# Decoder kernel: routing and scattering three of four token chunks inside the attention stream, expert tiles in fixed places, late expert weights on another queue, banded layer-norm gain applied elsewhere

## The chip, the core and the metric

The kernel runs on one core of one Trainium2 chip. The metric is the device time of one execution in microseconds (us); three executions of the kernel before were timed. TensorE (PE) multiplies matrices from SBUF into PSUM, VectorE (DVE) and ScalarE (ACT) do elementwise work and reductions, GpSimd (POOL) does elementwise work and issues the indirect transfers, SyncE (SP) issues the other transfers. PEld is PE's weight load. Each engine runs its own list of instructions in order; engines wait for one another by semaphores.

## The reference

Two decoder layers over 2048 tokens of width 256, each with self-attention, cross-attention over a context of 1601 tokens, a feed-forward block, and a layer norm after each. What matters here is the end of the first block, and the mixture of experts that closes the second layer.

```python
# layer 0, banded attention: layer norm with gamma and beta, then a GELU block
x = _layernorm(x + attn, gamma, beta)          # (x - mu) * rsqrt(var + eps) * gamma + beta
x = x + (gelu(x @ W1 + b1) @ W2 + b2)
...
# layer 1: mixture of 8 experts, the best 2 for every token
scores = x_flat @ gate_w + gate_b
topk_vals, topk_idx = jax.lax.top_k(scores, 2)
topk_probs = jax.nn.softmax(topk_vals, axis=-1)
h = jax.nn.relu(einsum('td,edf->etf', x_flat, w1) + b1[:, None, :])
y = einsum('etf,efd->etd', h, w2) + b2[:, None, :]
out = einsum('te,etd->td', combine_w, y)       # combine_w holds topk_probs
x = _layernorm(x + out)
```

Counted from the reference's inputs, its router sends 122, 34, 1250, 277, 133, 461, 1088 and 731 tokens to experts 0 to 7: 1, 1, 10, 3, 2, 4, 9 and 6 tiles of 128 rows, 36 in all.

## The kernel before

**Tiling.** Tokens stand in 16 tiles of 128 (`NT`), four tiles to a chunk (`QT`, `NQ` = 4). `x_tok` holds them row by row, `x_fm` column by column (features on the partitions). Stages follow one another as blocks, with a barrier of all engines between two blocks.

**Banded attention (layer 0).** At its end SP runs `behind(sp)`, here `clear_slots` (L2602): one transfer writes zeros into `x_slots`, which has 39 tiles of 128 rows in device memory (`EXPERT_TILES`). The block `close_attention` (L1006 to L1100) follows: product with `Wo`, residual, and a `RowNorm` (L222 to L260). On DVE `scale` normalises a tile (L239) and multiplies by gamma and adds beta (L243, L245); PE turns it (L252), ACT copies it to `x_fm` (L258). POOL adds the bias beforehand (L1037). The next block, `gelu_ffn`, loads its weights on SP (L1841 to L1844).

**The stream (`decoder_attention`).** Both attentions of layer 1 run as one stream of (score tile, key tile) pairs. `Plan` writes out its order by hand: `places` spreads the searches for row maxima (PE L1294, DVE L1307), which run 5 pairs ahead, `tasks[p]` holds the small jobs done after pair p, and `close_chunks` sets a chunk's closing jobs some pairs behind its last step. Products for maxima and all small jobs share a ring of four PSUM banks (`set_ring`); a product waits (`bank_free`) until the user four places earlier has been read. Per pair PE makes four score products (L1483), ACT their exponentials (L1624), PE the product with the values (L1499). The last 13 pairs have no maxima beside them. At the stream's start DVE and ACT wait for five loads (`s_w`, 80); POOL waits for `s_wo` and then prepares 16 residual tiles (L1692, L1695) before it does unit 0's cast (L1711), for which DVE waits at L1779.

**Routing and placing.** After the stream `route` (L1932 ff.) computes logits for 16 tiles (PE L1970, DVE L2001 to L2006) and the gates; SP loads the biases and `EARLY_EXPERTS` = 3 experts of 2 MB each. Then `place_tokens` (L2202 ff.) counts by prefix sums over 32 columns which slot each token takes (DVE chain L2251 to L2293, each link waiting for the one before), and POOL issues 32 indirect scatters of one column each (L2308) into `x_slots`; SP loads experts 3 to 7 meanwhile.

**Experts (`expert_ffn`).** 39 tiles in a hardware loop. For tile i SP loads 128 rows from `x_slots` (L2385), PE turns them (`turn_x`, L2413), multiplies by the first weight (`up`, L2424), turns (L2435) and multiplies by the second (`down`, L2443); DVE adds the bias (L2528), SP stores to `y_slots` (L2389). In one round SP issues load(i + 2) once `turn_x(i + 1)` is done and then waits for the bias of tile i to store it, so load(i + 3) stands behind that store. PE, ACT and DVE read the tile's expert number from SBUF into a register (`expert_of`, L2380). `up` waits for `s_resident`, which POOL raises expert by expert as the weights land. At the end POOL gathers both outputs of each token (L2503) and DVE sums them.

## Time and profile before

| | us |
|---|---|
| median of 3 runs | 3147.39 (3145.82 to 3147.58) |
| profiled execution, device time | 3147.17 |
| its span in the profile | 3145.4 |
| stream, first exponential to last copy into `x_fm` | 1298.8 to 2688.3 |
| routing and placing, up to the first row load | 2688.3 to 2769.5 |
| expert tiles, first `up` to last `down` | 2772.9 to 3090.9 |
| gather, sum, norm, output | 3091.0 to 3145.4 |

The profiled execution took 0.2 us less than the median. Its span is 1.8 us shorter than its device time, which holds what lies around it. The page gives PE as busy for 88% of the span, DVE 65%, ACT 52%, POOL 9%; these are averages over stages with different limits.

### The profile page before, as it was taken

How to read it: one execution, taken by the hardware profiler on the slowest of the kernel's cores; microseconds unless marked ns; L12 is line 12 of the kernel's file. 1: busy time of each engine (PE TensorE's matmuls, PEld its weight loads, DVE VectorE, ACT ScalarE, POOL GpSimd, SP SyncE). 2: the span in 40 equal slices, each digit the busy share in tenths (PEclk: the TensorE clock that was granted, in tenths of full speed). 3: DMA queues.
4: the chain of work that ended last, by engine and by line, in shares of the span. 5: the costliest groups of instructions: out<-in, count | busy, mean ns of one | idle time of the engine just before them, and what ended most of it. 6: DMA issues, size and time to landing. Idle time of an engine off the chain costs nothing. (4 is left out here: it accounts for less than half of the span.)

```text
span 3145.4 us, 85995 instructions
## 1 busy us (share of the span) xinstructions
PE 2774.2 (88%) x35706; PEld 1386.0 (44%) x35707; DVE 2054.1 (65%) x4240; ACT 1625.6 (52%) x3050; POOL 267.5 (9%) x381
## 2 busy tenths in 40 slices
PE   6796978999996988799999999999999999379992
PEld 3574643444543553233333333333343433247662
DVE  4444138888844236688898998989998994412224
ACT  2232213666662222277777777877777778023331
POOL 2113011000110001300000000000000000210003
PEclk9897988999997998699999999999999999589996
DMA  5412033011001004221212211111111110711112
GB/s 157 122 44 94 0 106 80 18 24 39 3 2 37 1 11 133 74 59 48 56 38 48 62 50 39 45 45 55 45 45 45 45 45 2 261 43 32 33 33 89
DMA packets 114947, 173.62 MB, mean 55 GB/s; under 512 B 19946, under 2 KB 90491, under 8 KB 114211
## 3 DMA queue, kind: packets, MB, share of 16 engines
q1 hardware_dynamic: 108772, 160.02, 17.8%
q0 software_dynamic: 5824, 8.49, 0.9%
q8 instruction: 272, 4.46, 0.6%
q14 instruction: 79, 0.65, 0.1%
HBM read 127.63 MB, written 40.51 MB: 53 GB/s over the span
## 5 line engine op out<-in xcount | busy, mean ns | idle before, releaser
L1307 DVE TENSOR_REDUCE d_part_max<-d_ps_m 128x1 f32<-128x512 f32 (+1 forms) x1964 | 1124.8, 630 | 86.4 <-PE d_ps_m L1294 53.3
L1624 ACT ACTIVATE d_prob<-d_ps_s 128x512 f32<-128x512 f32 x1856 | 960.2, 603 | 253.9 <-PE d_ps_s L1483 244.1
L1483 PE MATMUL d_ps_s<-q_st,k_st 98*32 98x512 bf16 x5104 | 445.2, 385 | 30.7 <-ACT d_prob L1624 28.8
L1294 PE MATMUL d_ps_m<-k_st,q_st 97*32 97x512 bf16 (+1 forms) x5296 | 471.9, 362 | 0.0
L698 DVE TENSOR_REDUCE x_part_max<-x_att_ps_m 128x1 f32<-128x512 f32 (+2 forms) x578 | 307.8, 586 | 43.3 <-PE x_att_ps_m L683 17.2
L939 ACT ACTIVATE x_att_prob<-x_att_ps_s 128x1024 f32<-128x1024 f32 (+3 forms) x296 | 258.2, 921 | 131.2 <-PE x_att_ps_s L820 78.2
L1499 PE MATMUL d_ps_o<-d_prob,a_values 128*32 128x512 f32 x2048 | 266.1, 595 | 0.0
L1483 PEld LDWEIGHTS d_ps_s<-q_st,k_st 98*32 98x32 bf16 x5104 | 136.3, 96 | 286.8 <-ACT d_prob L1624 182.6
L1294 PE MATMUL d_ps_m<-q_st 97*32 97x512 bf16 (+1 forms) x2560 | 227.6, 361 | 0.0
L1294 PEld LDWEIGHTS d_ps_m<-k_st,q_st 97*32 97x32 bf16 x5296 | 140.9, 96 | 178.8 <-issue 71.3
L1499 PE MATMUL d_ps_o<-d_prob,x_values 128*32 128x512 f32 x1664 | 215.3, 593 | 0.2 <-ACT d_prob L1624 0.2
L1483 PE MATMUL d_ps_s<-q_st 98*32 98x512 bf16 x2320 | 201.9, 382 | 8.6 <-ACT d_prob L1624 8.4
L674 PE MATMUL x_att_ps_m<-k_st,q_st 97*32 97x512 bf16 (+3 forms) x2312 | 203.5, 343 | 3.9 <-DVE x_part_max L698 3.0
L820 PE MATMUL x_att_ps_s<-q_st,k_st 98*32 98x512 bf16 (+3 forms) x2368 | 193.7, 357 | 12.0 <-DMA q_st<-x_neg_row 6.3
L2477 ACT ACTIVATE l1f_h_cols<-l1f_ps_t,l_b 128x128 f32<-128x128 f32 x312 | 84.7, 382 | 136.3 <-PE l1f_ps_t L2435 136.3
L2424 PE MATMUL l1f_ps_h<-l_w,l1f_x_cols 128*128 x312 | 143.3, 603 | 1.4 <-issue 0.7
L2443 PE MATMUL l1f_ps_y<-l_w,l1f_h_cols 128*128 x624 | 141.3, 379 | 2.2 <-ACT l1f_h_cols L2477 2.2
L853 PE MATMUL x_att_ps_o<-x_att_prob,v_grp 128*32 128x512 f32 (+3 forms) x1184 | 140.1, 543 | 0.4 <-ACT x_att_prob L939 0.4
L2522 DVE COPY l1f_h_rows<-l1f_ps_h 128x512 f32<-128x512 f32 x78 | 54.0, 692 | 127.3 <-PE l1f_ps_h L2424 127.3
L2443 PEld LDWEIGHTS l1f_ps_y<-l_w,l1f_h_cols 128*128 128x128 f32 x624 | 115.6, 190 | 17.0 <-issue 2.9
L1483 PEld LDWEIGHTS d_ps_s<-q_st 98*32 98x32 bf16 x2320 | 61.6, 96 | 120.7 <-ACT d_prob L1624 72.2
L1294 PEld LDWEIGHTS d_ps_m<-q_st 97*32 97x32 bf16 x2560 | 67.9, 96 | 86.7 <-issue 32.9
(328 smaller groups left out, 3342.5 us busy)
## 6 DMA issues: line engine op xcount, KB each, us to landing
k_st<-parts_k SPq DMA_DIRECT2D x90, 256.0 KB, 5.2
k_st<-parts_k SPq DMA_DIRECT2D x90, 208.0 KB, 4.7
l_w<-in_l_w SPq DMA_DIRECT2D x16, 1024.0 KB, 13.3
q_st<-parts_q SPq DMA_DIRECT2D x48, 256.0 KB, 4.7
q_st<-parts_q SPq DMA_DIRECT2D x192, 64.0 KB
q_st<-parts_k SPq DMA_DIRECT2D x30, 256.0 KB
q_st<-parts_k SPq DMA_DIRECT2D x30, 208.0 KB
parts_q<-a_proj_parts SPq DMA_DIRECT2D x16, 384.0 KB, 2.5
```

The source lines that it names most:

```text
L674: mm = pe.matmul(out[q:q + COLUMNS, :], q_st[0:rows, slot, j, start:start + COLUMNS], k_st[0:rows, slot, j, k:k + w], start=(half == 0), s ...
L698: dve.tensor_reduce(self.part[:, h * QT + a, i:i + 1], bank[:, 0:w], AX.X, ALU.max).then_inc(s_read, 1)
L820: mm = pe.matmul(bank[q:q + COLUMNS, hh, q0:QC], k_st[0:ROW_MAX + 1, bass.ds(slot(g), 1), h, key:key + COLUMNS], q_st[0:ROW_MAX + 1, bass. ...
L853: mm = pe.matmul(ps_o[32 * j:32 * j + 32, q0:QC], v_grp[:, kt, j, :], prob[:, k % 2, j, q0:QC], start=(i == 0), stop=(i == n - 1), skip_gr ...
L939: act.activation(prob[:, k % 2, 2 * u:2 * u + 2, q0:QC], bank[:, :, q0:QC], ACT.Exp, scale=scale).then_inc(s_prob, 1)
L1294: mm = pe.matmul(bank[q:q + COLUMNS, 0:w], self.query(s, h, ROW_MASK + 1, a * P + q, COLUMNS), self.key(s, h, ROW_MASK + 1, k, w), start=T ...
L1307: dve.tensor_reduce(self.part[:, h * QT + a, i:i + 1], bank[:, 0:w], AX.X, ALU.max).then_inc(s_read, 1)
L1483: mm = pe.matmul(ps_s[n % len(ps_s)][k:k + COLUMNS, :], maxima.key(s, h, ROW_MAX + 1, kt * P + k, COLUMNS), maxima.query(s, h, ROW_MAX + 1 ...
L1499: mm = pe.matmul(ps_o[32 * j:32 * j + 32, :], value_block(segments[si].values, kt, g * GH + j), prob[:, p % 2, j, :], start=(i == 0), stop ...
L1624: act.activation(prob[:, p % 2, h, :], ps_s[n % len(ps_s)][:, :], ACT.Exp, scale=scale).then_inc(s_prob, 1)
L2424: mm = pe.matmul(ps_h[hh][:, :], x_cols[:, m, :], w1_sb[:, bass.ds(e, 1), m, hh * QC:(hh + 1) * QC], start=(m == 0), stop=(m == DT - 1))
L2443: mm = pe.matmul(ps_y[:, 0:D], h_cols[:, f, :], w2_sb[:, bass.ds(e, 1), f, :], start=(f == 0), stop=(f == FT - 1))
```

## The change

- **Routing in the stream.** A class `Router` holds the gate weights and the counters. For chunks 0 to 2 the plan adds a `gate` task (PE logits of four tiles, DVE choice of two experts), three pairs later a `count` task (two products on PE, a prefix sum of 8 columns on DVE), and 8 `scatter` tasks on POOL, one every three pairs. The last chunk is done in a new block `dispatch` after the stream, with its 8 scatters. `route` and `place_tokens` go for layer 1.
- **Fixed places.** Each expert has 16 tiles of its own in `x_slots` (136 tiles with 8 spare ones, `SLOT_TILES`), so slots need no total. The zeros are written over 136 tiles. `expert_ffn` reads for each tile a row number from `tile_row` in SBUF, on SP, before each load and each store. Outputs go back into `x_slots`.
- **Weights.** SP loads experts 0 and 1 in `dispatch`. Experts 2 to 7 (12 transfers of 1 MB) are issued by POOL in `expert_ffn`, after the second row load has landed and before POOL raises `s_resident` for the first time.
- **Gain.** In the banded block PE turns the tile before gamma and beta. ACT applies them in its copy (two instructions of 128 columns, scale and bias per partition). POOL applies them to the rows with two operations per tile, after the turn. SP's zeros stand in its queue ahead of `gelu_ffn`'s weights, as before.
- **Waits.** In the stream DVE and ACT wait for `s_w` only at unit 0.

On PE, in the stream of the second attention, at the last chunk closed inside it. `x_tok` is turned for `x_fm` one job earlier; `d_ps_m` are the four ring banks. Before:

```order
L1294 MATMUL d_ps_m<-k_st,q_st 32x512 x4
L1509 MATMUL d_ps_m<-ident,d_o_raw 128x128 x4
L1483 MATMUL d_ps_s<-q_st 32x512 x4
...
L1499 MATMUL d_ps_o<-d_prob,x_values 32x512 x4
L1294 MATMUL d_ps_m<-k_st,q_st 32x128 x4
L1294 MATMUL d_ps_m<-k_st,q_st 32x512 x4
L1483 MATMUL d_ps_s<-q_st 32x512 x4
```

The same place in the changed kernel:

```order
L1313 MATMUL d_ps_m<-k_st,q_st 32x512 x4
L1663 MATMUL d_ps_m<-ident,d_o_raw 128x128 x4
L1637 MATMUL d_ps_s<-q_st 32x512 x4
...
L1653 MATMUL d_ps_o<-d_prob,x_values 32x512 x4
L1313 MATMUL d_ps_m<-k_st,q_st 32x128 x4
L1313 MATMUL d_ps_m<-k_st,q_st 32x512 x4
L1409 MATMUL d_ps_m<-router_w,x_fm 128x8 x8
L1637 MATMUL d_ps_s<-q_st 32x512 x4
```

Eight products for logits stand before the next pair's scores; the two count products stand three pairs later.

On SP, in the loop over the expert tiles, from the loop's start to its store. ISA and REGISTER_ALU are register instructions. Before:

```order
L2395 ISA
L2385 ISA
L2385 DMA l1f_x_rows<-x_slots 128x256
L2388 REGISTER_ALU
L2389 ISA
L2389 DMA y_slots<-l1f_y_rows 128x256
L2395 REGISTER_ALU
L2395 COMPARE_AND_BRANCH
```

In the changed kernel:

```order
L2568 ISA
L2546 TENSOR_LOAD l_tile_row
L2546 ISA x2
L2557 REGISTER_ALU
L2558 ISA
L2558 DMA l1f_x_rows<-x_slots 128x256
...
L2563 DMA x_slots<-l1f_y_rows 128x256
L2568 REGISTER_ALU
L2568 COMPARE_AND_BRANCH
```

A load from SBUF into a register and its two followers stand between the loop's start and the row load.

On POOL, in the expert block, before the gathers. In the changed kernel:

```order
L2486 DMA l_w<-in_l_w 128x2x1024
L2487 DMA l_w<-in_l_w 128x8x256
...
L2678 DMA l1f_y_two<-x_slots,router_slots 128x256 x32
```

Six such pairs of weight transfers stand there; before, POOL's list had only the 32 gathers.

The diff, cut to its core:

```diff
+SLOT_TILES = E * NT + E
@@ RowNorm
-            if self.gain is not None:
-                dve.wait_ge(self.s_x, 3 * t + 1)
-                dve.tensor_tensor(x, x, self.gain[:, 0, :], ALU.mult).then_inc(self.s_x, 1)
-                dve.wait_ge(self.s_x, 3 * t + 2)
-                dve.tensor_tensor(x, x, self.gain[:, 1, :], ALU.add).then_inc(self.s_x, 1)
+    def apply_gain(self, pool, t):
+        x = self.x_tok[:, t, :]
+        pool.wait_ge(self.s_turn, t + 1)
+        pool.tensor_tensor(x, x, self.gain[0][:, 0, :], ALU.mult).then_inc(self.s_gain, 1)
+        pool.wait_ge(self.s_gain, 2 * t + 1)
+        pool.tensor_tensor(x, x, self.gain[0][:, 1, :], ALU.add).then_inc(self.s_gain, 1)
...
+            for m in range(DT):
+                done = act.activation(self.x_fm[:, m, t * P:(t + 1) * P], self.ps[t % 2][:, m * P:(m + 1) * P],
+                                      ACT.Identity, scale=self.gain[1][:, 0, m:m + 1], bias=self.gain[1][:, 1, m:m + 1])
@@ Plan.close_chunks
+            if si == 1 and c < NQ - 1:
+                self.tasks[start + 14].append(("gate", c))
+                self.tasks[start + 17].append(("count", c))
+                for i in range(2 * QT):
+                    self.tasks[start + 19 + 3 * i].append(("scatter", c, i))
@@ Router, on VectorE: choose after the logits, place after the counts
+        dve.tensor_tensor(self.logit[:, :, :], bank[:, 0:self.LOGITS].rearrange("p (a e) -> p a e", e=E), ...
+        link(*(dve.max(self.best[:, a, :], self.logit[:, a, :]) for a in range(QT)))
+        link(*(dve.max_index(self.index[:, a, :], self.best[:, a, :], self.logit[:, a, :]) for a in range(QT)))
...
+        while w < C:
+            dst = self.upto[:, side, :, :]
+            link(dve.tensor_copy(dst[:, 0:w, :], src[:, 0:w, :]),
+                  dve.tensor_tensor(dst[:, w:C, :], src[:, w:C, :], src[:, 0:C - w, :], ALU.add))
@@ dispatch, on GpSimd
             pool.wait_ge(s_slots, 1)
-            pool.wait_ge(s_zero, 16)
-            for c in range(C):
-                pool.indirect_dma_start(x_slots, bass.IndirectOffsetOnAxis(slots[:, c:c + 1], 0),
-                                        x_tok[:, c // 2, :], None).then_inc(s_scatter, 16)
+            for i in range(2 * QT):
+                router.scatter(pool, c, i)
-EARLY_EXPERTS = 3
+EARLY_EXPERTS = 2
@@ expert_ffn
+        def rows(queue, dram, i):
+            row = queue.value_load(tile_row[0:1, bass.ds(i, 1)], min_val=0, max_val=SLOT_TILES - 1)
+            return dram[bass.ds(row * P, P), :]
...
             with sp.Fori(0, N - 2) as i:
-                sp.wait_ge(s_xturn, i + 2)
-                load(i + 2)
+                load(i + 2, i + 2)
                 store(i)
...
             pool.sem_inc(s_y, 1)
             pool.sem_inc(s_stored, 16)
+            pool.wait_ge(s_row, 32)
+            load_late(pool)
             for e in range(E):
                 pool.wait_ge(s_expert[e], 32)
                 pool.sem_inc(s_resident, 1)
@@ clear_slots
-                         cst["zeros"][:, :].rearrange("p (o n) -> p o n", o=1).to_broadcast((P, EXPERT_TILES, D)))\
+                         cst["zeros"][:, :].rearrange("p (o n) -> p o n", o=1).to_broadcast((P, SLOT_TILES, D)))\
```

## Rows read from the trace of the kernel before

**Rows 1.** Timeline after the stream: start, us, engine, line, operation, names, count, idle before
```profile
2687.03 1.24 ACT L1647 ACTIVATE x_fm<-d_ps_m 128x256 f32<-128x256 f32 x3 [0.19 <-PE d_ps_m L1544]
...
2693.04 13.82 PE L1970 MATMUL l1r_ps<-l1r_w,x_fm 128*128 128x8 f32 x64 [5.19 <-DMA l1r_b<-in_l_gate_b]
...
2725.87 1.06 POOL L2308 DMA_INDIRECT x_slots<-x_tok,l_slots  x1 [11.55 <-issue]
...
2765.46 0.97 POOL L2308 DMA_INDIRECT x_slots<-x_tok,l_slots  x1 [0.30 <-issue]
2769.45 10.68 SPq L2385 DMA_DIRECT2D l1f_x_rows<-x_slots  x3
...
2772.94 6.42 PE L2424 MATMUL l1f_ps_h<-l_w,l1f_x_cols 128*128 x8 [0.68 <-ACT l1f_x_cols L2468]
```

**Rows 2.** Timeline, small DVE operations of routing and placing, same columns
```profile
2694.20 0.17 DVE L2001 TENSOR_TENSOR l1r_logit<-l1r_ps,l1r_b 128x8 f32<-128x8 f32 x1 [3.53 <-PE l1r_ps L1970]
2694.40 0.17 DVE L2004 MAX8 l1r_best<-l1r_logit 128x8 f32<-128x8 f32 x1
...
2718.48 0.20 DVE L2260 COPY l1p_upto<-l1p_upto 128x64 f32<-128x64 f32 x1
```

**Rows 3.** Transfers that POOL issues, by line: duration ns min/median/max, first and last start
```profile
L709 POOL DMA_DIRECT2D q_st<-x_neg_row x56: 518/518/536, 544.4 to 887.0; - x56
L2308 POOL DMA_INDIRECT x_slots<-x_tok,l_slots x32: 965/969/1065, 2725.9 to 2765.5; - x32
```

**Rows 4.** Windows: us, busy us (instructions) of each engine, granted clock, DMA share, GB/s
```profile
core 0: us, PE busy (x) PEld busy (x) DVE busy (x) ACT busy (x) POOL busy (x), PEclk, DMA share, GB/s
2575.00:2611.00 36.00, 36.00 (x581) 14.53 (x577) 34.12 (x69) 27.97 (x56) 0.00 (x0) 1.00 0.12 33
...
2693.00:2713.00 20.00, 13.82 (x64) 13.72 (x64) 14.50 (x101) 0.32 (x1) 0.00 (x0) 0.50 1.01 361
```

**Rows 5.** Waits in 2575 to 2611: us in total, times, longest
```profile
PEld d_ps_m L1294 <- DVE d_part_max L1307: 3.8, 12, 0.4
```

**Rows 6.** Timeline, expert tiles: two turns of rows, SP's store and load
```profile
2784.63 0.14 PEld L2413 LDWEIGHTS l1f_ps_x<-ident,l1f_x_rows 128*128 128x128 f32 x1 [0.24 <-issue]
...
2789.74 0.37 SPq L2389 DMA_DIRECT2D y_slots<-l1f_y_rows  x1
...
2790.66 0.34 SPq L2385 DMA_DIRECT2D l1f_x_rows<-x_slots  x1
...
2792.81 0.37 PEld L2413 LDWEIGHTS l1f_ps_x<-ident,l1f_x_rows 128*128 128x128 f32 x2 [0.44 <-issue]
...
2793.04 0.38 PE L2413 MATMUL l1f_ps_x<-ident,l1f_x_rows 128*128 128x128 f32 x2
```

**Rows 7.** Line L2380 in 2793 to 2795.5, DVE's sequencer reads an expert number
```profile
L2380 DVEq TENSOR_LOAD <-l_tile_expert x1: 325/325/325, 2793.5 to 2793.5; - x1
...
L2380 DVEq SEQ_ASSERT  x1: 23/23/23, 2794.0 to 2794.0; - x1
```

**Rows 8.** Transfers in 236 to 276 (KB each, us to landing), then timeline
```profile
x_slots<-zeros SPq DMA_DIRECT2D x1, 4992.0 KB, 16.2
...
239.19 0.41 SPq L2602 DMA_DIRECT2D x_slots<-zeros  x1
...
252.80 0.42 DVE L243 TENSOR_TENSOR z_tok<-z_tok,a_gain 128x256 f32<-128x256 f32 x1
...
288.73 0.38 SPq L1841 DMA_DIRECT2D f_w<-in_f_w  x1
...
295.48 30.16 PE L1863 MATMUL f_psh<-x_fm,f_w 128*128 128x512 f32 x64 [7.42 <-DMA f_b<-in_f_b]
```

**Rows 9.** Timeline at the stream's start
```profile
1298.77 2.06 ACT L1624 ACTIVATE d_prob<-d_ps_s 128x512 f32<-128x512 f32 x4 [7.17 <-DMA d_vb<-in_x_bv]
...
1303.45 0.61 POOL L1692 TENSOR_TENSOR x_tok<-x_tok 128x256 f32<-128x256 f32 x1 [10.84 <-DMA d_bo<-in_x_bo]
...
1326.49 0.69 DVE L1779 TENSOR_TENSOR d_parts<-d_rest,d_parts 128x512 bf16<-128x512 f32 x1 [7.05 <-POOL d_parts L1711]
```

More of the change, by code:

```diff
@@ L1037, in _ @@
                 pool.tensor_tensor(dst[:, t, :], src[:, t, :], bo_sb[:, :], ALU.add).then_inc(s_base, 1)
+            if gain is not None:
+                for t in range(NT):
+                    norm.apply_gain(pool, t)
         @block.tensor
@@ L1221, in set_ring @@
             self.order += [("out", s) for s in range(len(self.steps)) if self.out_at[s] == p]
-            self.order += [task for task in self.tasks[p] if task[0] in ("turn", "prod", "fm", "unit", "v")]
+            self.order += [task for task in self.tasks[p] if task[0] in ("turn", "prod", "fm", "unit", "v", "gate", "count")]
         self.index = {step: r for r, step in enumerate(self.order)}
@@ L1353, in decoder_attention, with dve_links, link @@
+def dve_links(dve, s_chain):
+    links = 0
+    def link(*made):
+        nonlocal links
+        for instruction in made:
+            instruction.then_inc(s_chain, 1)
+            links += 1
+        dve.wait_ge(s_chain, links)
+    return link
+def decoder_attention(nc, name, plan, maxima, router, q_st, x_tok, x_fm, ctx_fm, t, cst):
     segments = plan.segments
@@ L1392, in decoder_attention @@
         s_store = [sem(f"store{i}") for i in range(2)]
+        s_gate_w, s_const, s_logits, s_taken, s_gates, s_counts, s_ranked, s_slots, s_chain = map(
+            sem, ("gate_w", "const", "logits", "taken", "gates", "counts", "ranked", "slots", "chain"))
         block = ctx.enter_context(nc.Block())
@@ L1469, in bank_free @@
                     pe.wait_ge(s_vout, user[1] + 1)
+                elif kind == "gate":
+                    pe.wait_ge(s_taken, user[1] + 1)
+                elif kind == "count":
+                    pe.wait_ge(s_ranked, user[1] + 1)
             def maxima_products(place):
@@ L1565, in unit_product, with gate_logits, gate_counts @@
                 mm.then_inc(s_mm, 1)
+            def gate_logits(step):
+                c = step[1]
+                pe.wait_ge(s_gate_w, 32)
+                pe.wait_ge(s_xfm, QT * (NQ + c + 1))
+                bank_free(step)
+                router.logits(pe, c, plan.bank(step), s_logits)
+            def gate_counts(step):
+                pe.wait_ge(s_const, router.CONSTANTS)
+                pe.wait_ge(s_gates, 2 * (step[1] + 1))
+                bank_free(step)
+                router.counts(pe, plan.bank(step), s_counts)
             def v_product(step):
@@ L1607, in _ @@
                         v_product(task)
+                    elif task[0] == "gate":
+                        gate_logits(task)
+                    elif task[0] == "count":
+                        gate_counts(task)
         @block.scalar
@@ L1699, in _ @@
             pool.memset(segments[1].values[:, :], 1.0).then_inc(s_ones, 1)
+            router.constants(pool, s_const)
             pool.wait_ge(s_wo, 64)
@@ L1811, in _ @@
                         add_value_bias(task)
+                    elif task[0] == "gate":
+                        choose(task)
+                    elif task[0] == "count":
+                        place_chunk(task)
 def gelu_ffn(nc, name, x_tok, z_tok, x_fm, w1, b1, w2, b2, cst):
@@ L2270, in _ @@
             link(dve.tensor_reduce(tiles[:, :], over[:, :, :], AX.X, ALU.add))
[L2271 removed]
+            link(dve.tensor_copy(end[:, 0:1], tiles[:, 0:1]),
+                  dve.tensor_scalar(spare[:, :], tiles[:, :], -1.0, float(NT), ALU.mult, ALU.add))
             for e in range(1, E):
                 link(dve.tensor_tensor(end[:, e:e + 1], end[:, e - 1:e], tiles[:, e:e + 1], ALU.add))
[L2274 removed]
@@ L2478, in relu @@
                                    bias=b1_sb[:, bass.ds(e, 1), f]).then_inc(s_hcol, 1)
+            act.activation(top[:, :], router.gap[:, :], ACT.Exp).then_inc(s_top, 1)
             copy_x(0, first=True)
@@ L2570, in decoder_kernel @@
         cst = constants(sb)
+        s_scatter = nc.alloc_semaphore("l1_scatter")
+        router = Router(sb, x_tok, x_fm, x_slots, s_zero, s_scatter)
         shared = ctx.enter_context(ExitStack())
@@ L2638, in decoder_kernel @@
                     StepAhead(nc, "a1_proj", plan, maxima, q_st, cst), cst, values[0][:, :])
-            decoder_attention(nc, "d1", plan, maxima, q_st, x_tok, x_fm, t["ctx_fm"], t, cst)
+            decoder_attention(nc, "d1", plan, maxima, router, q_st, x_tok, x_fm, t["ctx_fm"], t, cst)
         shared.close()
```

287 lines of the change are left out of this document (184 added, 103 removed).

## Prediction

> **What bounds the kernel now.** I read the timeline from the end of the stream to the first expert tile first, since that is where the change takes work away. The last chunk's copies into `x_fm` end at 2688.3, and the first `up` starts at 2772.94 [rows 1]: 84.6 us between stream and experts. In it PE waits 5.2 us for the gate bias and makes logits for 13.8 us, the DVE chain follows, and 32 scatters run from 2725.87 to 2765.46, one every 1.27 us (0.97 and a gap of 0.30). The row load comes 3.0 us after the last one has been issued.
>
> Then the windows inside the stream, where that work goes. In 2575 to 2611 PE is busy for all 36.00 us, DVE for 34.12, POOL for nothing [rows 4], and the weight loads for the maxima wait 12 times for DVE's search, 3.8 us in all [rows 5]: PE and DVE both bound, POOL free. In the expert loop PE turns the next tile's rows at 2792.81, 0.44 us after its last load, where its natural gap is 0.24 [rows 6]: the landing of SP's row load, issued at 2790.66 and so 0.9 us behind the store, gates it, with at most 0.1 us to spare. The last views are the close of the banded block and the start of the stream [rows 8, 9].
>
> **Tail: -53.6 us.** The last chunk's routing in the changed kernel: PE starts about 1.2 us after 2688.3, at 2689.5; 16 logit instructions at 13.82/64 = 0.216 us (half clock, 0.50 in the window [rows 1, 4]) take 3.5 us, to 2693.2 with the drain. The choice is 13 small DVE operations at a pitch of about 0.19 (2694.20 to 2694.40 is 0.20 [rows 2]), 2.45 us, to 2695.7; two count products, 1.3 us with their waits, to 2697.0; `place` is 14 operations at 0.20, 2.8 us, to 2699.8. POOL starts 0.9 later at 2700.7 and its eight scatters take 7 x 1.27 + 0.97 = 9.9, to 2710.6. With the 3.0 us of before, and 0.6 for SP's register load (below), the first row load is issued at 2714.2 instead of 2769.45. Turn and second load follow as before (3.5 us from load to `up`), but POOL needs the second load's landing, at 2719.2. The first `up` could then start at 2719.3 instead of 2772.94: -53.6.
>
> **The late weights: +15.3 and +3.** New between this landing and the first `up` are 12 transfers of 1 MB that POOL issues before it raises `s_resident`. Queued behind them on POOL is the first permission for `up`, and so every expert tile; SP waits behind the first bias. The trace has no such transfer. POOL's plain one with four rows costs 0.52, its indirect one with 128 rows 0.97, each with a gap of 0.30 [rows 1, 3]. Low bound: 12 x 0.82 = 9.8. I take the indirect row, the one that is nearest in descriptors: 12 x 1.27 = 15.3. High bound: the 0.45 us between the two rows put down to 124 more rows is 3.6 ns for each; then `w1` with 256 pieces costs 1.4, `w2` with 1024 pieces 4.2, and six pairs with gaps come to 6 x (1.4 + 4.2 + 0.6) = 37, or 40 when `w1` and `w2` also read their indices as slowly as the indirect row does. The Trainium skill ("DMA: Bandwidth & Descriptors", "Anatomy of one DMA, SWDGE (gpsimd) path") says that many descriptors can be emitted before the incremental cost shows; by it the value would be near the low end. No row here shows it.
>
> These 12.6 MB at 361 GB/s [rows 4] keep the DMA engines busy for 35 us, over the first four tiles. Each row load there may come later: +3, from 0 (they share no queue) to 12 (3 us on each of four). Expert 2 is needed at the third tile, 16 us on, and is the first of the late ones: in time.
>
> **The stream: +14.5.** Three chunks bring DVE 3 x (2.45 + 2.8) = 15.8 us in linked operations, PE 3 x (16 x 0.108 at full clock + 0.6) = 7.0. DVE has 36.00 - 34.12 = 1.9 us idle in 36, PE nothing. The ring of four banks lets PE run on for a pair at most, and it already waits for DVE. Low 8: PE's own work and little more, DVE's hidden in its idle time. High 24: both add, with the extra waits for a bank. I take 14.5, DVE's work less what one ring hides (0.4 a chunk, the longest wait of [rows 5]). The 24 scatters are hidden: POOL is idle there, and each has three pairs. Gate and count of the third chunk lie near 2590, ahead of the last maxima, so none falls in the 13 free pairs.
>
> **The expert loop: +18.** SP reads a row number before each load. DVE's sequencer takes 0.325 for such a read, its check ends 0.52 after the read began, and one register operation follows [rows 7]: 0.6. The read stands ahead of the wait for the turn, but behind the store, and the load is gated by the store (0.9 behind it [rows 6]), so nothing covers it except 0.1 us. Turn, and with it `down`, the bias, and the next store, move by 0.5 in every round: 36 x 0.5 = 18. Low 11 (0.3 each, the read alone), high 29 (0.8, if SP is slower by half). The read before a store is done ahead of its wait and costs nothing. The Trainium skill ("DMA: Bandwidth & Descriptors", "Latency and other measured facts") gives `tensor_load` a floor of about 600 ns, against 325 in the row; by the page the term would be +29 and the whole 3155.6.
>
> **Banded block: 0.** DVE loses two operations of 0.42 a tile [rows 8], over 13 us in all, and POOL gains two a tile; the block ends some 10 us earlier, near 278. But the zeros stand ahead of the feed-forward weights on SP. 4992 KB landed in 16.2 us, 308 KB a us; 17408 KB take 56.5 us from 239.2, to 295.7, or 48 at the 361 of [rows 4], to 287.5. The weights then want up to 6.8 us (288.73 to 295.48), partly beside the zeros. PE would start between 285 and 300, before at 295.48: I take 0, range -10 to +4. So the zeros take the place of the wait removed. ACT's second copy a tile lies beside PE's turn.
>
> **Start of the stream: 0.** ACT and DVE no longer wait 7 us for the value bias. POOL, though, waits 10.84 us for `bo` until 1303.45, prepares 16 tiles, and casts only then; DVE waits for that at 1326.49 [rows 9]. These times stay, only DVE's stall there grows from 7 to 14. The router's constants, 19 short operations on POOL, lie in its 10.84 us.
>
> **Sum.** -53.6 + 15.3 + 3 + 14.5 + 18 + 0 = -2.8. Against the profiled execution's 3147.2 this gives 3144.4 us; that execution lies 0.2 under the median.
>
> **Rivals.** (A) Slower: the cost of a late transfer grows with its pieces, as between the two rows of POOL's transfers. The 12 then take 37 to 40 instead of 15.3, the first `up` comes after 2756, and the sum is +22: 3169. It decides from about 24 us for the 12 (over 2.0 us each), where the sum passes +6. For it: the two rows differ by just that; against: an indirect transfer also reads indices, which a plain one does not. The skill's sentence quoted above speaks against it. (B) SP's read is hidden: a row load lands earlier than the turn needs it, or SP reads while its store still waits. For it: the gap of 0.44 exceeds the natural one by only 0.2. The loop adds nothing: 3126. Against: [rows 6] shows the load 0.9 behind the store. (C) The feed-forward weights don't queue behind the zeros, but share the engines with them. FFN starts at about 285: 3134. Against: one queue, and 20 MB in all must move in any case. (D) The change doesn't do what it says: the scatters of the stream wait for one another and end behind it. 24 of them need 31 us of 3 x 170; no.
>
> **How the numbers follow.** Forecast, with its own range of 3133 to 3158: 0.54. (A) 3169: 0.25. (B) 3126: 0.12. (C) 3134: 0.07. (D) and the rest: 0.02. A measurement tells 0.2% from no change, here 6.3 us: faster is under 3141.1, slower over 3153.7. The forecast's share divides into 0.19, 0.27 and 0.08; with B and C the chance of faster is 0.38, of the same 0.27, of slower 0.35 with A and the rest. The range of 8 in 10 reaches to B's lower and A's upper side: 3123 to 3172.
>
> **What would show it.** Right: an `up` some 15 us after the second row load's landing, and about 50 us of tail gone; each of the three chunks' stretches about 5 us longer with PE still at its limit; a tile period of 8.5 instead of 8.0, with the gap before `turn_x` near 0.9; FFN's first product near 295 with a wait for its weights; DVE's stall at L1779's successor near 14 us. Wrong: POOL's late transfers at over 2 us each (A), an unchanged tile period (B), FFN before 288 (C), a stream that is longer by over 24 us, or third and later tiles whose `up` waits for `s_resident` or for rows that land late.

## The result and the profile after

The changed kernel takes 3172.28 us (median of 4 runs, 3165.03 to 3173.34) against 3146.61 (4 runs, 3145.43 to 3147.58): 1.008 times as long, with an interval of 1.0068 to 1.0093. It is 25.7 us slower. The prediction was 3144.4, with a range of 3123 to 3172 and a chance of 0.38 for faster: the time lies on the other side, just above the range's upper end.

The profiled execution took 3172.37 us, its span is 3170.5, 25.1 more than before. Where each stage ends:

| | before, us | after, us | difference so far |
|---|---|---|---|
| first feed-forward product of layer 0 starts | 295.48 | 296.17 | +0.7 |
| row maxima of the stream's second step found | 1341.78 | 1342.28 | +0.5 |
| last copy into `x_fm` ends | 2688.3 | 2731.2 | +42.9 |
| first row load issued | 2769.45 | 2755.55 | -13.9 |
| first `up` | 2772.94 | 2765.80 | -7.1 |
| last `down` ends | 3090.9 | 3115.9 | +25.0 |
| span | 3145.4 | 3170.5 | +25.1 |

The tail gave 50.0 us, as the change meant it to. The stream took 42.4 back, and the expert tiles another 32.1. The timeline after the stream, answering to [rows 1] (start, us, engine, line, operation, names, count, idle before and what ended it):

```profile
2732.46 3.55 PE L1409 MATMUL l1p_ps_logits<-router_w,x_fm 128*128 128x8 f32 x16 [1.64 <-PEq L109]
...
2742.31 0.97 POOL L1468 DMA_INDIRECT x_slots<-x_tok,router_slots  x1 [103.53 <-DVE router_slots L1462]
...
2751.51 0.97 POOL L1468 DMA_INDIRECT x_slots<-x_tok,router_slots  x1 [0.30 <-issue]
...
2755.55 16.84 SPq L2558 DMA_DIRECT2D l1f_x_rows<-x_slots  x3
...
2760.73 0.80 POOL L2486 DMA_DIRECT2D l_w<-in_l_w  x1 [8.25 <-DMA l1f_x_rows<-x_slots]
2761.52 0.97 POOL L2487 DMA_DIRECT2D l_w<-in_l_w  x1
...
2765.66 0.75 POOL L2486 DMA_DIRECT2D l_w<-in_l_w  x1
2765.80 5.86 PE L2596 MATMUL l1f_ps_h<-l_w,l1f_x_cols 128*128 x8 [7.47 <-POOLq L2672]
...
2769.54 0.98 POOL L2487 DMA_DIRECT2D l_w<-in_l_w  x1
```

From the stream's end to the first row load it is 24.3 us where 81.2 were. `w1` takes POOL 0.80, `w2` with four times the pieces 0.97, and PE waits 7.47 for POOL. The twelve rows of POOL run without gaps from 2760.73 to 2770.52, 9.8 us. PE's first `up` starts at 2765.80 all the same, while POOL's seventh row has just begun: the permission left POOL's sequencer (POOLq) at 2765.6, 5.1 us after the first row and 4.9 before the last one ends, although it stands behind all twelve in POOL's list.

The stream first. DVE closes a step's search with one operation, L1310 before and L1329 after, so the distance of two such rows is the length of a step. There are 32 steps, numbered from 0; the second step is number 1. In the kernel before, second attention, timeline of DVE:

```profile
2291.95 0.22 DVE L1310 TENSOR_REDUCE d_neg_max<-d_part_max 128x16 bf16<-128x64 f32 x1
...
2327.30 0.22 DVE L1310 TENSOR_REDUCE d_neg_max<-d_part_max 128x16 bf16<-128x64 f32 x1
```

In the changed kernel, the same two steps, with rows of POOL, DVE, ACT and PE between them:

```profile
2297.80 1.06 POOL L1468 DMA_INDIRECT x_slots<-x_tok,router_slots  x1 [154.21 <-DVE router_slots L1462]
...
2299.23 0.22 DVE L1329 TENSOR_REDUCE d_neg_max<-d_part_max 128x16 bf16<-128x64 f32 x1
...
2301.30 0.60 ACT L1797 ACTIVATE d_prob<-d_ps_s 128x512 f32<-128x512 f32 x1 [1.09 <-remote]
...
2306.33 0.69 DVE L1326 TENSOR_REDUCE d_part_max<-d_ps_m 128x1 f32<-128x512 f32 x1 [4.56 <-remote]
2306.84 0.97 POOL L1468 DMA_INDIRECT x_slots<-x_tok,router_slots  x1 [0.30 <-issue]
2307.74 0.60 ACT L1797 ACTIVATE d_prob<-d_ps_s 128x512 f32<-128x512 f32 x1 [5.85 <-remote]
2308.39 0.11 PEld L1637 LDWEIGHTS d_ps_s<-q_st,k_st 98*32 98x32 bf16 x4 [6.28 <-issue]
...
2342.64 0.22 DVE L1329 TENSOR_REDUCE d_neg_max<-d_part_max 128x16 bf16<-128x64 f32 x1
```

The step lasts 43.41 us instead of 35.35. Two things are to be seen. The eight scatters stand in 10 us (2297.80 to 2306.84, every 1.27), not one in three pairs: the plan puts them at a distance of three pairs, but POOL has nothing else in its list, and the waits that stand before each scatter (for the tile's rows and for the chunk's slots) are all met already when the first one goes. And 4.1 us after the first of them ACT, DVE and PE stand for 4.6 to 6.3 us, with "remote" or "issue" as what ended it, which is to say that the profile names no instruction of this kernel. The same picture is there twice more: ACT stands for 7.28 us until 2473.69 and for 7.24 until 2640.28, and each time it stops 4.1 us after the first scatter (2462.28, 2628.88).

| chunk | growth up to the first scatters (choice, counts, places), us | growth with and behind them, us |
|---|---|---|
| 0 | 5.3 | 8.1 |
| 1 | 3.6 | 10.0 |
| 2 | 5.3 | 8.7 |

That is 41.0; the border between the columns is good to a us or two. The other 1.5 us arise ahead of the chunks, in the first four steps; several of the runs below with the same code there lack them, so they are put down to the spread between executions.

The expert tiles. SP and PE in the loop, timeline, answering to [rows 6]:

```profile
2791.32 0.68 PE L2585 MATMUL l1f_ps_x<-ident,l1f_x_rows 128*128 128x128 f32 x2 [4.64 <-DMA l1f_x_rows<-x_slots]
...
2801.16 0.43 PE L2585 MATMUL l1f_ps_x<-ident,l1f_x_rows 128*128 128x128 f32 x2 [0.31 <-DMA l1f_x_rows<-x_slots]
...
2809.84 0.43 PE L2585 MATMUL l1f_ps_x<-ident,l1f_x_rows 128*128 128x128 f32 x2 [0.33 <-DMA l1f_x_rows<-x_slots]
...
2814.72 0.36 SPq L2563 DMA_DIRECT2D x_slots<-l1f_y_rows  x1
...
2816.41 0.34 SPq L2558 DMA_DIRECT2D l1f_x_rows<-x_slots  x1
```

A tile takes 8.68 us (2801.16 to 2809.84) instead of 7.98, and from a store to the next row load it is 1.69 us instead of 0.92. PE now waits for the rows in nearly every tile, about 0.3 us each, and once, for the fourth tile, 4.64 us. SP's sequencer in 2860 to 2870, by line (duration ns min/median/max):

```profile
L2546 SPq FUSED_REGOPS  x5: 43/152/159, 2860.0 to 2868.9; - x5
L2546 SPq TENSOR_LOAD <-l_tile_row x3: 262/263/437, 2860.1 to 2868.6; - x3
```

The banded block and the stream's start, answering to [rows 8, 9], first the row of the transfers (KB, us to landing), then the timeline:

```profile
x_slots<-zeros SPq DMA_DIRECT2D x1, 17408.0 KB, 53.8
...
278.72 6.97 SPq L2040 DMA_DIRECT2D f_w<-in_f_w  x1
...
296.17 14.04 PE L2062 MATMUL f_psh<-x_fm,f_w 128*128 128x512 f32 x25 [22.05 <-DMA f_b<-in_f_b]
...
1325.58 0.69 DVE L1959 TENSOR_TENSOR d_parts<-d_rest,d_parts 128x512 bf16<-128x512 f32 x1 [16.65 <-POOL d_parts L1887]
```

SP comes to the weights 10 us sooner (278.72, before 288.73), and PE gets them no sooner. DVE begins earlier and waits 16.65 us for POOL where it waited 7.05.

### The profile page after: what moved, and what is told of

The parts are those of the page before. It is cut to its first block and busy times, and to the rows that moved or that the text cites. A ratio compares the mean times of both kernels' runs of the same rounds, so it can differ in the third digit from the quotient of the medians.

```text
span 3170.5 us, 86395 instructions
## 1 busy us (share of the span) xinstructions
PE 2789.9 (88%) x35718; PEld 1375.6 (43%) x35719; DVE 2045.6 (65%) x4209; ACT 1633.6 (52%) x3066; POOL 301.8 (10%) x441
## 5 line engine op out<-in xcount | busy, mean ns | idle before, releaser
L1637 PE MATMUL d_ps_s<-q_st,k_st 98*32 98x512 bf16 x5104 | 446.0, 386 | 36.1 <-ACT d_prob L1797 28.5
L2704 DVE TENSOR_TENSOR l1f_y_rows<-l1f_ps_y,l_b 128x256 f32<-128x256 f32 x39 | 16.6, 424 | 156.3 <-PE l1f_ps_y L2615 156.3
## 6 DMA issues: line engine op xcount, KB each, us to landing
x_slots<-zeros SPq DMA_DIRECT2D x1, 17408.0 KB, 53.8
```

Source lines behind the costliest of these rows:

```text
L1637: mm = pe.matmul(ps_s[n % len(ps_s)][k:k + COLUMNS, :], maxima.key(s, h, ROW_MAX + 1, kt * P + k, COLUMNS), maxima.query(s, h, ROW_MAX + 1 ...
```

## The experiments

Each kernel starts from the changed one. The kernel before was timed again beside them: its median is 3147.05 us beside the edits that put the scatters behind the stream, spread them, read row numbers ahead or put the zeros behind the weights; 3148.27 beside bursts of three, one at a time, experts 0 and 1 first and the four edits; 3147.26 beside plain transfers, paced weights and the late chain; 3145.33 beside one in each pair. One execution can differ from the next of the same code by some us as early as the stream's start, so stages are compared within a run.

### Scatters behind the stream

```diff
-                for i in range(2 * QT):
-                    self.tasks[start + 19 + 3 * i].append(("scatter", c, i))
@@ dispatch
+            for chunk in range(NQ):
+                for i in range(2 * QT):
+                    router.scatter(pool, chunk, i)
```

> Changed kernel with all 32 scatters issued in the block after the stream; choosing and placing of chunks 0 to 2 stay in the stream. Theory A (the burst of eight scatters on POOL stalls PE, ACT and DVE, about 8 us in each of three chunks; DVE's chains cost the other 5.3 each): the steps with scatters lose their +8.1, +10.0 - 3.6 and +8.7 us, the stream ends near 2707 instead of 2731, and the tail grows by 24 x 1.27 = 30.5 us; total about 3172.3 - 24 + 30.5 = 3179. Theory B (the chains on DVE make the whole 41 us, the stall only falls together with the scatters): the stream ends near 2731 still, total about 3203.

Measured: 3173.03 us, 1.0083 (1.0066 to 1.0100) times the kernel before. From the maxima of step 17 to those of step 31, the last, the stream grew by 15.4 us instead of 41.0. The tail took the scatters back: 32 rows of POOL from 2711.61 to 2751.36, and from the stream's end to the first row load 56.0 us instead of 24.3. So the chains on DVE cost about 15 us (17.0 in their own three steps; one step ahead of them was 1.7 shorter) and the scatters in the stream about 26, against 31.7 behind it. Theory A is the nearer one, 6 us over the measured time; theory B is 30 over it. That the total is almost the changed kernel's is a coincidence: the tail lost 31.7, the stream gave 28.5, of which 1.5 in a step that differs between executions anyway, and the stream's second step came 2.2 us earlier.

### Scatters really spread

```diff
                         pool.wait_ge(s_slots, task[1] + 1)
+                        pool.wait_ge(s_pv, p - 1)
```

> Changed kernel; POOL waits before each scatter of the stream for the product with the values two pairs earlier, so that scatters really come one in three pairs (some 7 us apart) and not eight in 10 us. Theory A1 (the stall comes from the burst: it begins 4.1 us after the first scatter, at the fourth, and the first three cost nothing): no stall, stream -24 us, total about 3148. Theory A2 (each scatter stops the other engines for about 1 us wherever it stands): the stream keeps its 43 us of growth, in small pieces, total about 3172. Theory C (a coincidence with the transfer of the row maxima, which is issued near the same time): at most one stall in three goes or stays; total between 3148 and 3172.

Measured: 3144.89 us, 0.9996 (0.9986 to 1.0006). 27.4 us less than the changed kernel, for one wait. POOL's timeline, and DVE's rows of maxima for the two steps in which the changed kernel stood:

```profile
2296.50 1.06 POOL L1468 DMA_INDIRECT x_slots<-x_tok,router_slots  x1 [154.78 <-PE d_ps_o L1653]
2305.65 0.98 POOL L1468 DMA_INDIRECT x_slots<-x_tok,router_slots  x1 [8.09 <-PE d_ps_o L1653]
2313.46 0.97 POOL L1468 DMA_INDIRECT x_slots<-x_tok,router_slots  x1 [6.82 <-PE d_ps_o L1653]
```

```profile
2297.34 0.22 DVE L1329 TENSOR_REDUCE d_neg_max<-d_part_max 128x16 bf16<-128x64 f32 x1
...
2332.67 0.22 DVE L1329 TENSOR_REDUCE d_neg_max<-d_part_max 128x16 bf16<-128x64 f32 x1
```

The step lasts 35.33 us, as before the change. The stall is gone from all three chunks, and the growth that is left is 15.3 us, the chains'. Theory A1 holds; A2 falls, since the same 24 scatters now cost nothing; C falls, since the transfer of the row maxima is sent as before.

### Bursts of three

```diff
-                    self.tasks[start + 19 + 3 * i].append(("scatter", c, i))
+                    self.tasks[start + 19 + 9 * (i // 3)].append(("scatter", c, i))
@@ and the wait of the spread kernel
```

> Changed kernel with the scatters of a chunk in bursts of three, three and two, nine pairs apart. In the changed kernel ACT stops 4.10, 4.13 and 4.16 us after the first scatter of a burst of eight, which is after three scatters at a pitch of 1.27 (3.8 us). Theory D (the first three back to back cost nothing, the stall needs a fourth): as with one in three pairs, total 3145, no idle time of ACT over 2 us behind a burst. Theory E (any back-to-back issue costs its own time once the burst has begun): about 1 to 3 us at each of the nine bursts, total 3150 to 3165.

Measured: 3156.6 us, 1.0022 (1.0013 to 1.0032), 11.7 more than with spread scatters. ACT around the second burst of chunk 0 (2324.58, 2325.85, 2327.13):

```profile
2329.04 2.06 ACT L1797 ACTIVATE d_prob<-d_ps_s 128x512 f32<-128x512 f32 x4 [2.50 <-PE d_ps_s L1637]
```

In chunk 0 the two bursts of three made a step 3.2 us longer, the burst of two the next one 1.1. Theory E holds, and my reading of the 4.1 us as "the fourth scatter" falls: three back to back cost as well.

### One at a time

```diff
+                        if task[2] > 0:
+                            pool.wait_ge(router.s_scatter, 16 * (2 * QT * task[1] + task[2]))
```

> Changed kernel with the eight scatters of a chunk one behind the other, each issued only when the one before it has landed. Theory F (the stall comes from several scatters being under way at once): no stall, or a short one, total 3145 to 3150; the pitch of the scatters grows to about 3 us. Rival G (what counts is how many scatters POOL issues in a short time, or POOL's own work on their indices, under way or not): ACT still stands for several us in each chunk, total 3155 to 3172.

Measured: 3146.87 us, 0.9995 (0.9985 to 1.0005). POOL's timeline:

```profile
2291.60 1.06 POOL L1468 DMA_INDIRECT x_slots<-x_tok,router_slots  x1 [154.20 <-DVE router_slots L1462]
2294.93 0.98 POOL L1468 DMA_INDIRECT x_slots<-x_tok,router_slots  x1 [2.26 <-DMA x_slots<-x_tok,router_slots]
```

A scatter has landed 3.3 us after its start. With the wait for the landing the scatters of chunk 0 come every 3.2 to 5.1 us, and the steps that hold scatters grew by 0.6, 1.3 and 0.1 us in the three chunks instead of 8.1, 10.0 and 8.7. This agrees with theory F, but a slower pitch comes with it, so overlap and pitch are not yet told apart.

### One in each pair

```diff
-                    self.tasks[start + 19 + 3 * i].append(("scatter", c, i))
+                    self.tasks[start + 19 + i].append(("scatter", c, i))
@@ and the wait of the spread kernel
```

> Changed kernel; the eight scatters of a chunk come one each pair, by a wait for the product two pairs back, beside the maxima. A pair lasts 2.2 to 2.7 us there, a scatter 3.2 us from its start to the next one that waits for its landing, so two are under way most of the time, at a pitch twice that of the burst (1.27). Theory F (a scatter issued while another is under way stops the others): seven such in a chunk, 4 to 8 us of stall in each of three chunks, total 3157 to 3170. Theory J (it needs the burst's pitch, that is, scatters issued faster than they go; two under way cost nothing, as in the last pairs of the kernel with the late chain, where none stalled at a pitch of 2.18): step length 35.3 to 35.9 us as with spread scatters, total 3145 to 3148.

Measured: 3142.11 us, 0.9985 (0.9976 to 0.9995). POOL's timeline:

```profile
2303.51 0.97 POOL L1468 DMA_INDIRECT x_slots<-x_tok,router_slots  x1 [1.64 <-PE d_ps_o L1653]
2306.17 0.97 POOL L1468 DMA_INDIRECT x_slots<-x_tok,router_slots  x1 [1.69 <-PE d_ps_o L1653]
2308.83 0.97 POOL L1468 DMA_INDIRECT x_slots<-x_tok,router_slots  x1 [1.69 <-PE d_ps_o L1653]
```

At a pitch of 2.66 us two scatters are under way, and nothing stands: no idle time of ACT over 1.35 us beside the scatters, growth of the stream from step 17 on 15.3 us. Theory F falls, J holds: two under way are free, a pitch of 1.27 us is not. With 3.3 us to land, a pitch of 1.27 also puts a third one under way, so whether the pitch or the third one counts was not separated.

### Plain transfers in the same burst

```diff
-                        router.scatter(pool, *task[1:])
+                        n = 2 * QT * task[1] + task[2]
+                        pool.dma_start(router.x_slots[n * P:(n + 1) * P, :], x_tok[:, n // 2, :])
+                            .then_inc(router.s_scatter, 16)
```

> Changed kernel; the 24 scatters of the stream are replaced by plain transfers that POOL issues at the same places, each of the same 128 rows to a fixed tile of x_slots. The tokens of chunks 0 to 2 so do not reach their experts; amount of data, tiles and everything else are the same. Theory H (several transfers of POOL under way at once are enough to stop the other engines, whatever their kind): 1 to 8 us at each of the three bursts, total 3155 to 3172. Theory I (it takes indirect ones, whose 128 row addresses POOL works out one by one): no stall, stream growth 16 us as with spread scatters, total about 3145.

Measured: 3143.82 us, 0.999 (0.9981 to 0.9999). POOL, in the row of the timeline:

```profile
2283.20 4.33 POOL L1896 DMA_DIRECT2D x_slots<-x_tok  x8 [153.86 <-DVE router_slots L1462]
```

This kernel leaves out the scattering of chunks 0 to 2. Eight plain transfers of the same 128 KB go out in 4.33 us, faster than the indirect ones, and the step lasts 35.35 us (2284.93 to 2320.28), as before. The traces give both kinds 384 packets and 1.05 MB for a burst. Neither the bytes nor the number of transfers makes the stall; of the kinds tried it takes indirect ones at their own pitch. The result is theory I's. Its reason, that POOL works out 128 row addresses, is not shown: the plain transfers also write rows that lie next to one another, and no run tells that from the kind of the transfer.

### Row numbers read ahead

```diff
+            load(2, 2)
+            with sp.Fori(0, N - 3) as i:
+                target = rows(sp, token_slots, i)
+                source = rows(sp, token_slots, i + 3)
+                sp.wait_ge(s_y, i + 2)
+                sp.dma_start(target, y_rows[:, :]).then_inc(s_stored, 16)
+                sp.wait_ge(s_xturn, i + 3)
+                sp.dma_start(x_rows[:, :], source).then_inc(s_row, 16)
```

> Changed kernel; in the expert loop SP reads both row numbers (of the store and of the next load) before it waits for the bias of the tile, so that no register load stands between a store and the next row load. Theory (the read behind the store is what lengthens each tile from 7.98 to 8.67 us): tile period back to about 7.98, 35 x 0.69 = 24 us less, total about 3148. Rival (the row load lands late because its address is computed, or because x_slots is read and written in one tensor): the period stays above 8.5, total about 3170.

Measured: 3146.29 us, 0.9993 (0.9983 to 1.0002), 26.0 less than the changed kernel. SP's timeline:

```profile
2857.91 0.36 SPq L2573 DMA_DIRECT2D x_slots<-l1f_y_rows  x1
2858.52 0.34 SPq L2575 DMA_DIRECT2D l1f_x_rows<-x_slots  x1
2865.89 0.36 SPq L2573 DMA_DIRECT2D x_slots<-l1f_y_rows  x1
```

From store to load 0.61 us instead of 1.69, and a tile every 7.98 us. The number reads between the store and the next row load were the whole of the 0.7 us a tile. The theory holds.

### Zeros behind the weights

```diff
-                      clear_slots)
-            gelu_ffn(nc, "f0", ..., cst)
+            gelu_ffn(nc, "f0", ..., cst, clear_slots)     # issued behind w2
```

> Changed kernel; the zeros are issued on SP behind the feed-forward weights instead of ahead of them. Theory (the zeros of 17.8 MB hold back the weights and eat what the shorter banded close gave): the first feed-forward product at about 286 instead of 296.2, total about 3162. Rival (the weights themselves or the barrier set that time): the first product stays within 2 us of 296, total about 3172.

Measured: 3163.96 us, 1.0056 (1.0039 to 1.0073), 8.3 less. The first feed-forward product:

```profile
289.67 10.62 PE L2063 MATMUL f_psh<-x_fm,f_w 128*128 128x512 f32 x20 [11.84 <-DMA f_b<-in_f_b]
```

It starts 6.5 us sooner than in the changed kernel; SP issued the weights at 282.41 there, later than the 278.72 of the other execution, and the forecast of 286 was not reached. The theory holds: what the shorter block gave went into the queue behind the zeros.

### Experts 0 and 1 let go first

```diff
+            for e in range(EARLY_EXPERTS):
+                pool.wait_ge(s_expert[e], 32)
+                pool.sem_inc(s_resident, 1)
             pool.wait_ge(s_row, 32)
             load_late(pool)
-            for e in range(E):
+            for e in range(EARLY_EXPERTS, E):
```

> Changed kernel; POOL lets experts 0 and 1 go (their weights have landed long before) ahead of issuing the twelve late transfers. In the changed kernel PE waits 7.47 us for POOL there, and then 4.64 us for the rows of the fourth tile. Theory (POOL's issuing is on the path): the first product with the first weight 7 us sooner, total about 3165. Rival (the rows of the third and fourth tile land no sooner, as the late weights fill the DMA engines, and PE waits for them instead): the wait for rows grows by as much, total within 2 us of 3172.

Measured: 3172.19 us, 1.0076 (1.0055 to 1.0097), the same as the changed kernel. PE's timeline:

```profile
2756.54 5.60 PE L2596 MATMUL l1f_ps_h<-l_w,l1f_x_cols 128*128 x8 [0.68 <-ACT l1f_x_cols L2640]
...
2782.28 0.68 PE L2585 MATMUL l1f_ps_x<-ident,l1f_x_rows 128*128 128x128 f32 x2 [4.67 <-DMA l1f_x_rows<-x_slots]
2782.76 6.07 PE L2615 MATMUL l1f_ps_y<-l_w,l1f_h_cols 128*128 x16
...
2796.32 0.43 PE L2585 MATMUL l1f_ps_x<-ident,l1f_x_rows 128*128 128x128 f32 x2 [3.19 <-DMA l1f_x_rows<-x_slots]
```

The wait of 7.47 for POOL is gone, the one of 4.64 stays, and one of 3.19 is new. From the first row load to the last `down` it is 356.1 us instead of 360.3: of the 6.9 us gained at the first tile 2.7 came back in the next ones. Whether the other 4.2 are a gain in the total stays open: the profiled execution took 3167.82 us, 4.5 less than the changed kernel's, but the four runs go from 3166.07 to 3177.04, and their median is the same. The theory's 7 us was not reached; the rival has the wait for rows right and gives back more than the trace shows.

### Four edits together

Spread scatters, row numbers read ahead, zeros behind, experts 0 and 1 first.

> Changed kernel with four edits together: scatters one in three pairs, both row numbers read ahead of the bias wait, zeros behind the feed-forward weights, experts 0 and 1 let go first. If the stages are independent the gains add up: 3172.3 - 27.4 - 26.0 - 8.3 = 3110.6, and up to 7 less by the last edit, 3104 to 3111. Rival (SP's earlier row loads, or the earlier start, run into the late weights, and a part is given back): 3112 to 3125.

Measured: 3112.2 us, 0.9883 (0.9867 to 0.9900). The sum of the parts was 3110.6, with nothing for the last edit; 1.6 us over it is inside the spread of the changed kernel's own runs, so the stages add up within what can be told. By its number the time lies at the rival's lower edge (3112), and up to 7 us by the last edit did not come. The tiles from first `up` to last `down` still take 332.8 us against 317.9 before, all of it beside the late weights.

### Late weights paced

```diff
-EARLY_EXPERTS = 2
+EARLY_EXPERTS = 3
@@ expert_ffn, on GpSimd
+            for e in range(EARLY_EXPERTS, E):
+                pool.wait_ge(s_row, 16 * (2 * (e - EARLY_EXPERTS) + 3))
+                load_late(pool, e, 0)        # w1
+                pool.wait_ge(s_row, 16 * (2 * (e - EARLY_EXPERTS) + 4))
+                load_late(pool, e, 1)        # w2
```

> As the four edits together (3112.2), but three experts are loaded early, and the ten late transfers of 1 MB are issued one at a time, each when a tile's rows have landed, from the third tile on. In the kernel with four edits PE waits 4.40 and 4.51 us for the rows of the fourth and fifth tile, and three products with the second weights take 5.4 to 6.3 us instead of 3.6, 332.8 us in all from first to last product against 317.9 of the kernel before. Theory (the late weights crowd out rows and instructions in one lump of 35 us): the waits fall under 1 us, 10 to 14 us less, total 3098 to 3102. Rival (any weight transfer beside a tile delays its rows): ten waits of 1 to 2 us take the place of the two long ones, total 3105 to 3115.

Measured: 3099.8 us, 0.9849 (0.9835 to 0.9862), 12.4 less. PE's timeline, tiles two to four:

```profile
2729.62 3.69 PE L2604 MATMUL l1f_ps_h<-l_w,l1f_x_cols 128*128 x8 [0.65 <-issue]
...
2737.70 3.60 PE L2604 MATMUL l1f_ps_h<-l_w,l1f_x_cols 128*128 x8
...
2745.69 3.60 PE L2604 MATMUL l1f_ps_h<-l_w,l1f_x_cols 128*128 x8
```

A tile every 7.99 us from the start, no wait for rows, and 318.7 us from the first `up` (2721.93) to the last `down` (3040.6), against 317.9 before and 350.1 in the changed kernel. A transfer of 1 MB fits between the landing of one tile's rows and the issue of the next; twelve in a lump don't. The edit changes two things, the pace and a third expert loaded early, and no run parts them. The early expert has a price: from the stream's end to the first row load it is 27.4 us, where the kernel with four edits has 24.3.

### The last chain where DVE stands idle

```diff
+                last = c == NQ - 2
+                gate = self.total - 12 if last else start + 14
+                self.tasks[gate].append(("gate", c))
+                self.tasks[gate + 3].append(("count", c))
+                for i in range(2 * QT):
+                    self.tasks[gate + 5 + (1 if last else 3) * i].append(("scatter", c, i))
```

> As the kernel with paced weights, and the choice, the counts and the scatters of chunk 2 are moved into the last 12 pairs of the stream, where DVE has nothing to reduce and stands idle for 15.6 and 23.8 us; its scatters come one each pair, 2.2 us apart. Theory (a chain costs its 5.3 us only because DVE is the bound beside the maxima): stream 4 to 5 us shorter, total about 5 less than the paced kernel. Rival (scatters 2.2 us apart overlap, as one needs 3.2 us to land, and cost about 1 us each as in the bursts): 8 us of stall eat the gain, total 0 to 4 more than the paced kernel.

Measured: 3095.98 us, 0.984 (0.9827 to 0.9854), the fastest kernel here. From the second step's maxima to the first `up` it is 1385.9 us instead of 1389.3: 3.3 of the 5.3 us of that chain are saved. ACT runs through all the scatters there:

```profile
2656.30 0.97 POOL L1470 DMA_INDIRECT x_slots<-x_tok,router_slots  x1 [0.79 <-PE d_ps_o L1655]
2658.48 0.97 POOL L1470 DMA_INDIRECT x_slots<-x_tok,router_slots  x1 [1.21 <-PE d_ps_o L1655]
```

At a pitch of 2.18 us none of them stops anything, so the rival falls. The other 2 us are spent where the chain went: from the last step's maxima to the stream's end it is 57.8 us instead of 55.6. In the last pairs the chain is cheaper, not free.

## Why the prediction was wrong, step by step

**The scatters in the stream: the step that failed.** The prediction has "The 24 scatters are hidden: POOL is idle there, and each has three pairs." The second half is false, the first is no reason. The order of POOL's instructions could have told it: between two scatters POOL's list holds no wait that is still open, so a distance of three pairs in the plan is none in time. I had costed the burst only as POOL's own time. It stops PE, ACT and DVE and makes the stream some 8.6 us longer each time: 25.7 us in all (41.0 less the chains' 15.3). Without it (spread scatters) the changed kernel takes 3144.9. That this is the forecast's 3144.4 is partly luck: two other terms were wrong by 11 us each and cancel, as shown below.

**The chains in the stream: right.** Predicted +14.5, measured +15.3 (spread scatters; 15.4 with none in the stream).

**The tail: right.** First row load 25.9 us behind the stream's end predicted, 24.3 measured.

**POOL's issue of the late weights: mis-sized, to the good.** Taken +15.3 from the landing of the second row load to the first `up`, measured 5.1 (2760.73 to 2765.80; PE's wait of 7.47 also holds the time until that landing). Two things make the difference. The twelve rows take 9.8 us, the prediction's low bound, and not 15.3. And `up` did not wait for them all: the permission left POOL's sequencer while the rows of the last six were still to come, so "Queued behind them on POOL is the first permission" is right for the list and wrong for the rows. A transfer with 256 pieces took POOL 0.80 or less, one with 1024 pieces 0.98 or less. The price by pieces, 3.6 ns each, was wrong by more than ten times: 768 more pieces cost 0.2 us. An indirect transfer with 128 rows costs as much as a plain one with 1024 pieces, so the step from POOL's plain row to its indirect one was a step between kinds, not between numbers of rows. The trace agrees with the sentence of the Trainium skill ("DMA: Bandwidth & Descriptors", "Anatomy of one DMA, SWDGE (gpsimd) path") that many descriptors go out before their cost shows. Rival (A) falls with this: that its 3169 lies next to the measured 3172 is luck, for the twelve took 9.8 us where it has 37 to 40.

**Late weights beside the tiles: mis-sized.** Taken +3, measured some 7.5: the tiles took 32.1 us more, 24.6 of them are 36 times the longer period. They don't share SP's queue, but keep the DMA engines full (share 1.02 and 1.03 of 2770 to 2780 and 2780 to 2790, 0.50 in 2796 to 2799) until about 2798, some 37 us after the first was issued, and the row load of the fourth tile waits in them.

**The register read: right in kind, low in size.** Taken 0.5 a tile, measured 0.68 (36 tiles: 24.6 us, not 18). The read itself takes SP 0.26 to 0.28, less than the 0.325 of [rows 7] and well under the floor of 600 ns that the Trainium skill ("DMA: Bandwidth & Descriptors", "Latency and other measured facts") gives for `tensor_load`; the measurement decides. But with its register operations it put 0.8 us between store and load, the upper end of what I had. Rival (B) falls.

**Banded block and stream start: right.** Predicted 0 and 0, measured +0.7 and -0.2. The zeros took the place of the wait that was removed: they landed at 291.6 (53.8 us after 237.78), between the two bounds of 287.5 and 295.7. The lower bound mixes KB of 1024 bytes with GB of 10^9 and should be 288.6; the sum by the skill's floor is 3155.4 and not 3155.6. Neither changes anything. POOL's 16 preparations kept the start.

The predicted sum was -2.8, the measured one 25.1, so the miss is 27.9: 25.7 from the stall, 0.8 from the chains, 2.0 from the start, the first steps and the end, 11.1 from the tiles (32.1 for 21), less 11.7 from the tail with POOL's issue (-50.0 for -38.3). That the last two almost cancel is luck; because they do, the miss in time is the size of the stall.

## What to carry to other kernels

A place in a plan is a place in time only on an engine that is made to wait for the others. Where an idle engine gets jobs "one in three pairs", look in its list for what holds it back. Of a moved instruction ask not only what it costs its own engine, but whether the others keep running while it is issued; if the trace shows it only where they are idle, as here, that price is open on the slow side and belongs into the range. A gain that ends in a queue behind something larger (weights behind zeros, rows behind weights) is had by the order in the queue alone: the four small edits and the two after them turned +26 us into -51.

## What the runs showed of the hardware

Indirect scatters of 128 rows, issued by POOL back to back at 1.27 us, make ACT, DVE and PE stand while POOL itself goes on, and SP's one transfer is issued in the midst of it (2466.97 and 2634.09, after ACT had stopped). The stream grows by about 8.6 us for eight, 1 to 2 for two or three. At a pitch of 2.18 us or more nothing stands, even with two under way, and eight plain transfers of the same size in 4.33 us do nothing either. In the step with the stall the DMA engines are not the bound (windows view, 2299 to 2343: us, PE, PEld, DVE, ACT, POOL busy, granted clock, DMA share, GB/s):

```profile
core 0: us, PE busy (x) PEld busy (x) DVE busy (x) ACT busy (x) POOL busy (x), PEclk, DMA share, GB/s
...
2299.00:2343.00 44.00, 37.70 (x581) 14.86 (x577) 35.03 (x71) 27.72 (x53) 6.81 (x7) 0.92 0.21 64
```

The DMA share is 0.26 in 2302.5 to 2308.3, the stall alone, and PE's granted clock is 0.52 from 2308.3 to 2313, close to the lower of its two levels (1.2 of 2.4 GHz), after PE has stood; then it is 1.00 again. In that stretch four score products take 0.62 to 0.65 us where they took 0.38 to 0.40, which is part of the cost of a burst.

What the engines wait for could not be settled: the profile calls it "remote" or "issue". One rival can be looked at in the traces, that the engines stand because their instructions are loaded late beside the scatters. The DMA queue of kind "instruction" moves no packet in the stall of chunk 0 (2302.1 to 2308) nor in that of chunk 2 (2633 to 2641), and one in that of chunk 1, at 2468 to 2470, over 3 us before ACT goes on. This speaks against it; no run tested it. What indirect transfers share with the signals between the engines stays open too.
